# Edge attention in a graph kernel: the weighted rows are summed on TensorE, and ScalarE lays the gathered keys into PSUM

## The reference, cut to what matters

```
# layer 1: 4 heads of 64, softmax per destination node
mod_k  = K[src] + 0.2 * rel_w[edge_relations]
scores = einsum('ehd,ehd->eh', Q[dst], mod_k) / D ** 0.5
ex     = exp(scores - seg_max[dst]);  w = ex / segment_sum(ex, dst)[dst]
agg    = segment_sum(w * V[src], dst)
# layer 2: 8 heads of 32, key is k[src] + edge_attr @ We, softmax over all edges
alpha  = (q[dst] * (k[src] + e)).sum(-1) / sqrt(32)
out    = segment_sum(v[src] * softmax(alpha, axis=0), dst) + bias
```

## Time and profile before

| | |
|---|---|
| median of 3 runs | 4426.26 us |
| profiled execution: its own time | 4430.56 us |
| profiled execution: span | 4428.8 us |
| VectorE busy | 3253.1 us (73%) |
| GpSimd busy | 2983.3 us (67%) |
| TensorE busy | 2686.6 us (61%) |
| ScalarE busy | 719.6 us (16%) |
| mean granted TensorE clock | 0.788 of 2.4 GHz |

### The profile page before, as it was taken

How to read it: one execution, slowest core, us unless ns; L and a number is a source line. 1 busy time by engine, 2 the same in 40 slices (tenths; PEclk the granted TensorE clock), 3 DMA queues, 4 the chain that set the end, 5 groups by cost and what they waited for, 6 DMA issues and landing times. The chain is left out here.

```text
span 4428.8 us, 52906 instructions
## 1 busy us (share of the span) xinstructions
PE 2686.6 (61%) x11454; PEld 1433.4 (32%) x11454; DVE 3253.1 (73%) x7572; ACT 719.6 (16%) x2122; POOL 2983.3 (67%) x2929
## 2 busy tenths in 40 slices
PE   4244578888887799466666656578888853000007
PEld 4144332222222688233233334344444422000004
DVE  7497458888888233489999976499989986666664
ACT  0011100000000233233333322111111102000004
POOL 0577667777765577677777737677777745777772
PEclk8555799999999899777888878787888876555558
DMA  3235346666665333466666733376666643444441
GB/s 159 36 113 156 76 123 179 178 178 171 175 173 147 74 62 61 119 173 172 173 172 175 199 67 69 102 186 185 187 186 186 186 112 78 111 108 108 108 106 40
DMA packets 408930, 594.52 MB, mean 134 GB/s; under 512 B 267146, under 2 KB 273430, under 8 KB 407806
## 3 DMA queue, kind: packets, MB, share of 16 engines
q0 software_dynamic: 185552, 519.27, 42.8%
q1 hardware_dynamic: 223278, 74.01, 7.1%
HBM read 532.97 MB, written 59.26 MB: 134 GB/s over the span
## 5 line engine op out<-in xcount | busy, mean ns | idle before, releaser
L1106 POOL DMA_INDIRECT edge_ring<-tab,edge_rec x480 | 475.8, 991 | 146.2 <-issue 135.2
L1688 PE MATMUL edge_psX<-edge_w_edge,edge_featT 64*128 64x256 f32 x1920 | 440.6, 451 | 196.3 <-DVE edge_prod L1764 193.7
L2028 POOL DMA_INDIRECT state<-tab,edge_rec x480 | 453.8, 945 | 155.7 <-issue 145.9
L1693 PE MATMUL edge_psX<-state,ident 128*128 128x512 f32 x720 | 446.2, 753 | 113.9 <-DMA state<-tab,edge_feat 104.2
L1135 PE MATMUL edge_psX<-state,ident 128*128 x720 | 379.6, 637 | 135.3 <-DVE edge_ring L1163 135.3
L1618 POOL DMA_INDIRECT state<-tab,edge_rec x360 | 351.5, 976 | 159.1 <-issue 102.4
L1688 PEld LDWEIGHTS edge_psX<-edge_w_edge,edge_featT 64*128 64x128 f32 x1920 | 297.7, 216 | 465.5 <-issue 401.3
L1618 POOL DMA_INDIRECT state<-tab,edge_feat x360 | 352.0, 978 | 109.7 <-issue 103.9
L2201 PE MATMUL gate_psA<-ident,gate_w_nat 128*128 128x128 f32 x8 | 2.0, 428 | 632.1 <-DMA gate_w_nat<-in_L_gnn_W_ih 632.1
L1163 DVE TENSOR_TENSOR edge_ring<-edge_psX,edge_ring 128x1024 f32<-128x1024 f32 x240 | 293.8, 1224 | 73.3 <-PE edge_psX L1142 43.4
L781 POOL DMA_INDIRECT sorted_d<-update_row_out,update_row_idx x200 | 237.7, 1189 | 92.3 <-issue 59.4
(11 more groups left out here) (439 smaller groups left out, 6362.0 us busy)
## 6 DMA issues: line engine op xcount, KB each, us to landing
sorted_d<-state SPq DMA_DIRECT2D x7, 2380.0 KB
state<-src_rows SPq DMA_DIRECT2D x25, 562.5 KB
state<-low_rows SPq DMA_DIRECT2D x25, 562.5 KB
state<-tab,edge_rec POOLq DMA_INDIRECT x840, 3.0
edge_ring<-tab,edge_rec POOLq DMA_INDIRECT x600, 3.7
update_row_out<-in_edge_attr SPq DMA_DIRECT2D x40, 156.2 KB
edge_rec<-rec_d SPq DMA_DIRECT2D x364, 8.0 KB, 2.8
state<-tab,edge_feat POOLq DMA_INDIRECT x360, 3.7
```

Of the source, the lines that this page charges most:

```text
L1106: pool.indirect_dma_start(out=ring[:, k, s, :], out_offset=None, in_=S["tab0"][:, :], in_offset=bass.IndirectOffsetOnAxis(ap=rec[:, k, R_S ...
L1688: pe.matmul(psX[k % 2][:, s % 2, s // 2, :], featT[lo:lo + ED, k % 4, s // PAIR, :], w_edge[lo:lo + ED, :], start=(s < 2), stop=False, ski ...
L1693: last = pe.matmul(psX[k % 2][:, a, :, :], S["ident"][:, :], ring[k % RING].rearrange("p (c a) f -> p a c f", a=2)[:, a, :, 0:D], start=Fa ...
L2028: pool.indirect_dma_start(out=ring[:, k, s, :], out_offset=None, in_=S["tab3"][:, :], in_offset=bass.IndirectOffsetOnAxis(ap=rec[:, k, R_S ...
```

## The change

- The sum of the weighted rows goes from VectorE to TensorE. `halve` and both `add_half` are gone. `decay` still writes the scaled accumulator into PSUM (`so_far`), and `add_terms` adds the four weighted rows by four matmuls of 256 columns against the identity. ScalarE then copies the sum into the accumulator (`write_sum`).
- The gathered keys go into `psX` by two ScalarE copies of 512 columns (`lay_keys`), ahead of the edge matmuls, which now add onto them. TensorE's two identity matmuls per turn are gone. Five matmuls at the start of a layer mark the PSUM banks as written.
- The edge matmuls are issued as slots 0, 2 and then 1, 3. In both layers slots 0 and 2 now use rows 0 to 63 of the array, slots 1 and 3 rows 64 to 127. Before, layer 1 alternated 0, 1, 2, 3 between the two row halves, and layer 2 had all four in rows 0 to 63. Layer 2's copy of the transposed features is now two copies of half the size.
- VectorE's turn begins with the weighting and the decay, and only then comes the wait for `psX`.
- A ring slot is free once the weighting has read it, which wrote to the tile `terms`; seven of the eight record slots are released by it, the last by `write_sum`.

The diff, cut to its core:

```diff
@@ load (SyncE)
-                    sp.wait_ge(s_done[k], uses(t, q, RING))
+                    if k == RING - 1:
+                        sp.wait_ge(s_acc, t * AQ + (q + 2))
+                    else:
+                        sp.wait_ge(s_terms, t * (2 * AQ) + (2 * q + 1))
@@ ScalarE
+                def lay_keys(t, k):
+                    act.wait_ge(s_xr, t * AQ + (k + 1))
+                    act.wait_ge(s_g[k % RING], uses(t, k, RING) * (16 * QE))
+                    for a in range(2):
+                        act.activation(psX[k % 2][:, a, :, :], ring[k % RING].rearrange("p (c a) f -> p a c f", a=2)[:, a, :, 0:D], ACT.Copy).then_inc(s_keys, 1)
+
+                def write_sum(t, k, b):
+                    hold(act, s_sum, t * AQ + (k + 1))
+                    act.activation(blk(S["big"], b)[:, D:D2], so_far, ACT.Copy).then_inc(s_acc, 1)
...
+                act.wait_ge(s_open, 1)
...
                 with nc.Fori(0, n, engines=[act.engine], hint_back_edge=True) as t:
+                    b = block_of(RING - 1)
                     for k in range(AQ):
+                        lay_keys(t, k)
                         copy_features(t, k + TURNED)
                         if layer == 1:
                             one_hots(t, k + AHEAD)
+                        write_sum(t, k, b)
+                        if k < AQ - 1:
+                            b = block_of(k, t)
                         act.wait_ge(s_cat, t * AQ + (k + 1))
                         act.activation(w, cat[:, k % 2, :, :], ACT.Exp).then_inc(s_exp, 1)
+                write_sum(n, 0, block_of(RING - 1))
@@ TensorE
+                def add_terms(t, k):
+                    pe.wait_ge(s_terms, t * (2 * AQ) + (2 * k + 2 * RING))
+                    for s in range(QE):
+                        last = pe.matmul(so_far, S["ident"][:, :], terms[:, s, :], start=False, stop=(s == QE - 1), skip_group_check=True)
+                    last.then_inc(s_sum, 1)
...
                         pe.wait_ge(s_fT, t * AQ + (k + 2))
-                        pe.wait_ge(s_xr, t * AQ + (k + 1))
-                        for s in range(QE):
-                            lo = ED * (s % PAIR)
-                            pe.matmul(psX[k % 2][:, s % 2, s // 2, :], featT[lo:lo + ED, k % 4, s // PAIR, :], w_edge[lo:lo + ED, :],
-                                      start=(s < 2), stop=False, skip_group_check=True)
+                        for a in range(2):
+                            pe.wait_ge(s_keys, t * (2 * AQ) + (2 * k + a + 1))
+                            for s in range(a, QE, 2):
+                                lo = ED * (s % 2)
+                                last = pe.matmul(psX[k % 2][:, a, s // 2, :], featT[lo:lo + ED, k % 4, s // 2, :], w_edge[lo:lo + ED, :],
+                                                 start=False, stop=True, skip_group_check=True)
+                        last.then_inc(s_x, 1)
                         turn_features(t, k + TURNED)
-                        pe.wait_ge(s_g[k % RING], uses(t, k, RING) * (16 * QE))
-                        for a in range(2):
-                            last = pe.matmul(psX[k % 2][:, a, :, :], S["ident"][:, :],
...
+                        add_terms(t, k)
@@ VectorE, one turn
-                        dve.wait_ge(s_x, t * AQ + (k + 1))
                         step.put(dve.tensor_scalar(score[:, QE, :], m, 0.0, None, ALU.add))
+                        hold(dve, s_exp, t * AQ + (k + 1))
+                        weigh(t, k, (k - 1) % RING)
+                        decay(b_prev)
+                        dve.wait_ge(s_x, t * AQ + (k + 1))
                         dve.tensor_tensor(prod[:, :, :].rearrange("p (c a) d -> p a c d", a=2), psX[k % 2][:, :, :, :],
...
-                        step.until(weighted)
-                        halved = step.put(halve())
-                        dve.nop().then_inc(s_done[at], 1)
...
-                        summed = step.put(add_half(so_far, 0))
...
-                        step(add_half(acc, 1))
```

More of the change, by code:

```diff
@@ L1711, in halve @@
-                def halve():
-                    return dve.tensor_tensor(terms[:, 0:2, :], terms[:, 0:2, :], terms[:, 2:4, :], ALU.add)
-                def decay(acc):
-                    return dve.tensor_tensor(so_far.rearrange("p (h d) -> p h d", h=heads), acc.rearrange("p (h d) -> p h d", h=heads),
-                                             bc(w[:, QE, :], 2, [P, heads, hd]), ALU.mult)
-                def add_half(to, i):
-                    return dve.tensor_tensor(to, so_far, terms[:, i, :], ALU.add)
@@ L1721, in last_values @@
[L1721 to L1735 removed]
+                    dve.tensor_tensor(terms[:, :, :].rearrange("p s (h d) -> p s h d", h=heads), vals,
+                                      bc(w[:, 0:QE, :], 3, [P, QE, heads, hd]), ALU.mult).then_inc(s_terms, 1)
@@ L1748, in _ @@
                 dve.nop().then_inc(s_xr, 2)
-                for k in range(RING - 1):
-                    dve.nop().then_inc(s_done[k], 1)
+                dve.nop().then_inc(s_terms, 2 * (RING - 1))
+                dve.wait_ge(s_open, 1)
                 n = turns(dve)
@@ L1794, in _ @@
                 step = Chain(dve, s_v, n * CH + PRE)
-                last_values(step, n, 0, RING - 1, block_of(RING - 1))
+                b = block_of(RING - 1)
+                l = blk(S["l"], b)[:, 0:heads]
+                hold(dve, s_exp, n * AQ + 1)
+                weigh(n, 0, RING - 1)
+                decay(b)
+                step(dve.tensor_tensor(l, l, w[:, QE, :], ALU.mult))
+                step(dve.tensor_reduce(tot[:, :], w[:, 0:QE, :].rearrange("p r h -> p h r"), AX.X, ALU.add))
+                step(dve.tensor_tensor(l, l, tot[:, :], ALU.add))
+                dve.nop(nofuse=True)
         ph.close()
```

89 lines of the change are left out of this document (44 added, 45 removed).

## The result

| | before | after |
|---|---|---|
| median | 4427.11 us (4425.43 to 4430.25, 4 runs) | 4613.03 us (4604.11 to 4637.55, 4 runs) |
| ratio | | 1.0428, 95% interval 1.0387 to 1.0469 |
| profiled execution, span | 4428.8 us | 4602.3 us |
| VectorE busy | 3253.1 us | 3029.1 us |
| ScalarE busy | 719.6 us | 1099.7 us |

The changed kernel is slower by 186 us; the forecast was 4556, in a range of 4440 to 4650.

What follows compares the result with a forecast made beforehand. GpSimd was taken to bound layer 2 and scattering layer 1, VectorE close behind. Layer 1 +60, layer 2 +63 and ends 7 made 130 us onto 4430.6: 4561, 4556 as median; range 4440 to 4650.

Steps and rivals of the forecast that it cites:

- The closed chain: Per turn, exponential, key copies, edge matmuls, product, next exponential in series: 6.2 us in layer 1, 6.3 in layer 2.
- The clock: Edge matmuls at TensorE's low clock in 20% of turns, 1.6 of eight: 2.9 us an iteration, bounds 0 and 5.4.
- Both fit, barely.: At full clock, TensorE's sum with its copy and ScalarE's queue end about 5.5 us, before the scores at 6.0.
- The rival that charged the whole turn at the low clock: TensorE's loop decides: slow turns of about 10.2 us, 35% of turns, iteration 63 us, total 4790; chance 0.08.
- The head of the loop body: ScalarE's table load and a block number load ahead of the first key copy: 2.0 us an iteration, no drain counted.
- The ends: Work behind each loop +1 to +3 twice, opening matmuls about +4 in layer 1, -1 in layer 2: together +7.
- No difference: Rival: turn of 5.8 us without slow ones, GpSimd decides as before, only the ends cost: 4433; chance 0.08.
- Faster: Rival: same chain below 51 us an iteration, GpSimd's instructions shorten without VectorE's additions beside them: 4406; chance 0.07.
- Mild: Rival: middle border of the edge matmuls overlaps, clock stays up, iterations 50.9 and 51.7 us: 4449; chance 0.15.
- The signs: If right: VectorE busy 65 to 70%, waits for keys, GpSimd waiting for records in layer 2, iterations 54 to 56 us.
- the signs against: GpSimd without waits in layer 2, key copies off 0.59, edge matmuls under 1.99, or VectorE waiting for the exponential.
- C: Theory from the follow-up expectations: TensorE waits for ScalarE once per turn, its clock falls, its steps on the chain lengthen.

Runs made afterwards that it cites:

- the keys laid ahead: Changed kernel, with the key copies of turn k+1 issued ahead of turn k's sum copy and exponential: 4390.34 us, ratio 0.9911.
- the filled kernel: Changed kernel plus four matmuls per turn whose result nobody reads, behind the sum of weighted rows: 4429.58 us, ratio 1.0000.
- the two kernels without the closed key chain: Changed kernel with keys again added by identity matmuls, 4385.76 us; changed kernel with key copies issued a turn ahead, 4390.34 us.
- the disturbed comparison: First measurement of four follow-up kernels, in which the kernel before itself took 5446.04 us; all four were run again.
- the keys alone: Changed kernel with the sum back on VectorE, ScalarE still laying keys: 4609.62 us; with seven unused matmuls per turn added, 4447.80 us.
- the filled kernel before: Kernel before plus two matmuls per turn whose result nobody reads, behind the key matmuls: 4439.01 us, ratio 1.0027.
- the sum alone: Changed kernel with keys again added by identity matmuls, TensorE still adding the weighted rows: 4385.76 us, ratio 0.9902.

## Why the prediction was right, and where not

The direction and its first reason, the closed chain, held; the size was 130 us where 186 were measured, and it came that near only because two errors pointed opposite ways. By its steps:

- **The closed chain.** Its members came as forecast: a key copy 1.10 / 2 = 0.55, product to subtraction 2215.19 - 2211.99 = 3.20 and the exponential 0.03 behind it where nothing holds it. The edge matmuls were the exception. They took 1.65 against 1.99, and were taken for serial. By the row of the keys laid ahead in layer 1 they take 1.14 in the same order. The 1.65 is the first pair and then the wait for the second key copy (it ends at 2210.65, 0.47 after the first matmul's start). The Trainium skill (TensorEngine Tiling, Key Properties) says that different tiles can work in parallel; that trace agrees with its 1.14. A turn at the full clock is 5.80 us in layer 1, not 6.2 (5.89 and not 6.3 in layer 2, by the filled kernel's median): the estimate was 8 x 0.4 = 3.2 us an iteration too high.
- **The clock: the term that failed.** It was taken as a share of slow turns (20%, 2.9 us an iteration), on the edge matmuls alone. The change did not keep the clock's habits of before. Against the filled kernel's iterations without a slow turn (48.8 and 49.5), the changed kernel's 55.4 and 58.0 hold 6.6 and 8.5 us of clock, two to three times the term. It struck the edge matmuls in one turn of eight (9 of 73, 10 of 82), less often than the 1.6 of eight forecast, and the sum, for which nothing was taken, in two of three or more (48 of 72, 60 of 83).
- **"Both fit, barely."** This sum was made at the full clock alone (sum's copy done at 5.5, scores at 6.0), while the low clock was applied to the edge matmuls only. With a sum of 3.47 us the 0.5 of slack becomes 1.1 of lateness. The rows for it were there: 3.78 for 1024 columns at the low clock. The rival that charged the whole turn at the low clock (10.2 us) erred to the other side: in most turns the edges run at the high clock and the sum at the low one. Its argument against itself, that the clock should return while TensorE is busy, is not what the slices show: there the clock fell as the sum began and was back when TensorE idled.
- **The head of the loop body.** 2.0 was taken. In layer 2 the first key copy comes 2.24 later than behind an exponential without a head (3215.86 against 3213.49 + 0.13), and the edge matmuls behind it are at the low clock, 0.9 more. The copy starts where the table load ends (3214.57 + 1.28), so leaving out a drain behind the load was right.
- **The ends.** +7 was taken and -1.3 measured. The first product, behind the opening matmuls, came 1.7 us later, and the stretch between the layers gave that back.
- **Sum.** Layer 1 +60, measured +78; layer 2 +63, measured +97; ends +7, measured -1. The chain's surplus had hidden part of the clock's deficit: with the measured turn and the same clock term an iteration would come to 51.3 and 51.9, that is 12 us in each layer, and with the 7 the forecast would have been some 4457. That 4556 lies only 57 us short of the measured time is to that extent luck.
- **The rivals.** "No difference" named a turn of 5.8 without slow ones, 4433. That is the filled kernel, 4429.58. "Faster" named GpSimd's instructions shortening; they did (below), of no use at the low clock. In the filled kernel layer 2 is 10 us shorter than before (751.9 against 762.3), and the two kernels without the closed key chain got the rest. "Mild" had the clock stay up, and it doesn't stay up by itself.
- **The signs.** VectorE's share, the waits for keys, and GpSimd's waits for records in layer 2 (80.0 us in 20 waits of 3000 to 3600 us, none of this length before) were as forecast. The iterations of 54 to 56 us were met in layer 1 and passed in layer 2 (58.0). Two of the signs against came true too: edge matmuls clearly under 1.99, and VectorE waiting for the exponential as long as for the keys. They pointed at the right step.

Still open is why the clock falls in the midst of a working stretch. The runs show which kernels it falls in, and that filling or opening the chain keeps it up. They don't show the rule. Nor do they part the wait for ScalarE, which C names, from TensorE's idle time as such: filling and opening the chain change both. Nor is it explained why the changed kernel's runs spread over 33 us, when outside the disturbed comparison the others' spread is 1 to 19.

## What to carry to other kernels

When a change makes TensorE wait once a turn for an engine that waits for it in turn, do the sum twice, with all of TensorE's steps on the chain at either clock. Here the mean clock of before did not tell it (0.81 before, 0.80 after), and the loop with the keys alone stayed at the slow one. Taking work off TensorE can then gain next to nothing (4595 against 4613 us with three quarters of the sum gone), and three idle matmuls a turn were worth 4%. Better is to open the chain: issue the copy for the next turn ahead of the wait of this one.

## What the runs showed of the hardware

**The clock follows the loop's form, not its amount of work alone.** With the same instructions per turn it was 0.80 with the chain closed and 0.87 to 0.93 with it open. The opened turns are shorter too, so that pair alone leaves the share of time open. The kernel before is the better partner: it has as many matmul columns a turn as the opened one, and nearly its iterations (51.10 against 49.9 us in layer 2), yet 0.84 where the opened one has 0.93 (0.81 and 0.87 in layer 1). With the keys alone the clock was 0.50 over 500 us of layer 1.

**GpSimd's gathers are shorter in the kernels in which VectorE doesn't add the weighted rows.** The page's row of the gathers of layer 1, before and then in the changed kernel:

```profile
L1618 POOL DMA_INDIRECT state<-tab,edge_rec x360 | 351.5, 976 | 159.1 <-issue 102.4
```

```profile
L1619 POOL DMA_INDIRECT state<-tab,edge_rec x360 | 341.9, 950 | 164.7 <-issue 96.4
```

Layer 2 has 978 and 946 ns. Over all kernels it is 945 to 953 ns in every kernel without `halve` and `add_half`, and 957 to 978 in every one with them (the keys alone, filled or not, and the filled kernel before among these). The Trainium skill (GPSIMD Engine Reference, Specifications) says that GpSimd's SBUF interfaces are shared with VectorE, with contention where VectorE has two SBUF inputs, as `halve` has. The rows agree with that, but don't show it: `weigh` has two SBUF inputs as well and stays in every kernel, and no run leaves out `halve` alone. In the sum alone it is worth 1.06 us of 51.10 in an iteration that GpSimd decides.
